# A transformer megakernel on one Trainium2 core: the two local-attention layers as one pipeline over tiles, with the inverse norm taken by a power on GpSimd

## The reference

```python
def _layer(x, wqkv, qs, ksc, wo, lg, lb, w1, b1, w2, b2):
    h = shift_token(x)
    q, k, v = jnp.split(h @ wqkv, 3, axis=-1)       # then to 8 heads
    q = l2norm(q) * qs
    k = l2norm(k) * ksc
    q, k = rotary_xpos(q, k)
    o = local_attention(q, k, v)                    # windows of 64, each sees itself and the one before, softmax
    x = x + o @ wo
    h = shift_token(x)
    ...                                             # layer norm, gated MLP
```

## Time and profile before

| | |
|---|---|
| median of 3 runs | 3057.51 us (3056.97 to 3065.76) |
| the profiled execution, its own time | 3055.92 us |
| its span, first to last instruction | 3054.1 us |
| instructions | 46022 |
| mean granted TensorE clock | 0.847 of 2.4 GHz |

### The profile page before, as it was taken

One profiled execution on the slowest core, in us unless ns is written; L12 is line 12 of the kernel. 1 busy time (PEld: TensorE's weight loads), 2 busy tenths in 40 slices (PEclk: granted clock), 3 DMA queues, 4 the chain that ended last, 5 costly groups with the idle time before them and its releaser, 6 DMA issues.

```text
span 3054.1 us, 46022 instructions
## 1 busy us (share of the span) xinstructions
PE 2275.5 (75%) x17392; PEld 1277.1 (42%) x17392; DVE 1975.2 (65%) x4104; ACT 1416.0 (46%) x2537; POOL 560.6 (18%) x336
## 2 busy tenths in 40 slices
PE   4798588577779668767759948867767985885766
PEld 4576122254547412245546712225353751222545
DVE  5855696655674489565656568946566556966565
ACT  1333277264533347554623416746263332782544
POOL 0242000213043200041205300012212420003130
PEclk9999599778879879978779968978777985997878
DMA  3000200101000100010000020010100002001010
GB/s 132 1 1 1 74 16 9 28 6 26 11 9 1 53 22 19 8 27 11 21 17 1 1 69 19 7 22 16 22 17 8 1 1 74 16 9 30 5 26 18
DMA packets 52016, 65.13 MB, mean 21 GB/s; under 512 B 17696, under 2 KB 29216, under 8 KB 51264
## 3 DMA queue, kind: packets, MB, share of 16 engines
q1 hardware_dynamic: 48584, 56.18, 7.3%
q10 hardware_dynamic: 3192, 5.80, 0.6%
HBM read 25.19 MB, written 15.01 MB: 13 GB/s over the span
## 4 chain that ended last, share of the span: by engine, by line
PE 49%; DVE 23%; ACT 12%; DMA 6%; issue 5%; SPq 3%; POOL 2%; ACTq 0%; DVEq 0%; POOLq 0%
PE PS L1136 44%; DVE arena L971 9%; ACT arena L616 5%; DMA tmp<-xf 3%; ACT arena L571 2%; PE PS L1415 2%; PE PS L1154 1%; DVE s_at L1027 1%; DMA scr_k<-arena 1%; DVE tmp L996 1%; POOL arena L437 1%; DMA arena<-scr_k 1%; PE PS L1480 1%; SPq L344 1%; DVE arena L1044 1%
## 5 line engine op out<-in xcount | busy, mean ns | idle before, releaser
L1136 PE MATMUL PS<-arena 128*32 128x256 f32 (+4 forms) x10240 | 825.3, 356 | 204.4 <-DMA arena<-scr_k 75.3
L971 DVE TENSOR_REDUCE arena<-PS 128x1 f32<-128x512 f32 x1024 | 642.0, 684 | 101.7 <-PE PS L1136 101.7
L571 ACT ACTIVATE arena<-PS 128x1024 f32<-128x1024 f32 x512 | 515.6, 1033 | 306.7 <-PE PS L1136 306.7
L1136 PEld LDWEIGHTS PS<-arena 128*32 128x32 f32 (+4 forms) x10240 | 313.0, 124 | 714.9 <-DVE arena L971 282.9
L1136 PE MATMUL PS<-wqkv,arena 128*128 128x512 f32 x384 | 221.1, 730 | 65.4 <-ACT arena L602 56.2
L1136 PEld LDWEIGHTS PS<-w2e,arena 128*128 128x128 f32 x2048 | 246.0, 192 | 52.0 <-issue 51.7
L527 ACT ACTIVATE arena<-PS 128x512 f32<-128x512 f32 x256 | 150.7, 597 | 245.1 <-PE PS L1136 245.0
L1136 PE MATMUL PS<-w2e,arena 128*128 128x128 f32 x2048 | 246.8, 275 | 0.1
L616 ACT ACTIVATE arena<-PS,arena 128x128 f32<-128x128 f32 x512 | 230.0, 527 | 16.0 <-DVE arena L1079 16.0
L917 DVE TENSOR_TENSOR arena<-PS,arena 128x512 f32<-128x512 f32 x128 | 86.1, 689 | 213.2 <-PE PS L1136 212.8
L601 ACT ACTIVATE arena<-PS 128x1024 f32<-128x1024 f32 x64 | 65.5, 1023 | 325.1 <-DVE s_at L1027 248.5
(11 more groups left out here) (274 smaller groups left out, 3463.7 us busy)
## 6 DMA issues: line engine op xcount, KB each, us to landing
arena<-arena SPq DMA_DIRECT2D x120, 128.0 KB, 2.3
arena<-scr_k SPq DMA_DIRECT2D x28, 200.0 KB
arena<-scr_q SPq DMA_DIRECT2D x28, 192.0 KB
scr_q<-arena SPq DMA_DIRECT2D x16, 256.0 KB, 3.0
scr_k<-arena SPq DMA_DIRECT2D x16, 256.0 KB, 5.2
x_in<-in_x SPq DMA_DIRECT2D x5, 512.0 KB, 4.0
scr_q<-arena ACTq DMA_DIRECT2D x8, 256.0 KB, 4.9
scr_k<-arena ACTq DMA_DIRECT2D x8, 256.0 KB, 5.8
```

Source lines behind the costliest of these rows:

```text
L571: act.activation(pb[:, n % 8], pair(2 * (n % 2)), ACT.Exp).then_inc(S["p"], 1)
L971: dve.tensor_reduce(mxp[:, h % 2, j, t, hf:hf + 1], PS[:, ring_bank("mx", h, n), :], AX, ALU.max)\
L1136: return pe.matmul(o, w, v, start=start, stop=stop, **kw)
```

## The change

The two phases become one loop of steps j. In step j the engines work on the projections of tile j+3, the norms and transposes of tile j+2, the scores of tile j+1, the exponentials of tile j, the division and transposition of j-1, and the output of j-3; j runs from -3. The PSUM banks are shared otherwise: scores have the one pair 0, 1, q and k the one pair 2, 3, v bank 4, the transposes of q, k and of the probabilities banks 5 and 6 in turn, output and projection bank 7. `qT` is held for two tiles, `pl` for two, `qk_a` for two and `qk_sq` for one. ACT copies both halves of the transposed probabilities. SP's two loops become one; `vz` has a semaphore for each tile, and `qk_ps` is new, so SP clears eight more semaphores at the end of an item.

The inverse norm of one tile is taken by one POOL instruction (sum to the power -0.5, 16 values per partition; the exponent comes from `sc[:, 11:12]`, set once), and DVE refines it with one Newton step. ACT's square root and DVE's reciprocal go, so do ACT's table loads for the square root (one per layer) and, in layer 0, the one for the exponential (the stage before ends in exponentials).

The diff, cut to its core:

```diff
-        qT = take([4, N])
-        after = used[0]
-        pl = take([3, 2, 4, KEYS])
+        pl = take([2, 2, 4, KEYS])
         pt = take([2, 2, 4, P])
+        hT = take([N])
+        qk_a = [take([2 * INNER]) for _ in range(2)]
+        qk_sq = take([2 * INNER])
         olT = x_in[:].rearrange("p (q c) n -> p q c n", c=4)
-        part = [take([2 * INNER], F32, after + i * 2 * INNER) for i in range(4)]
-        hT = take([N], F32, after + 4 * 2 * INNER)
-        flat = [v[:].rearrange("p t w -> p (t w)") for v in (tmp, x_in, s_at, tmp2)]
-        qk_a = part[0:2] + flat[0:2]
-        qk_b = flat[2:4]
-        qk_sq = part[2:4]
...
+                    for j in range(-3, T):
+                        t, u = j + 2, l * T + j + 2
+                        if 0 <= t < T:
+                            pool.wait_ge(S["ssq_ok"], u + 1)
+                            pool.tensor_tensor(rq[:, t], ssq[:, t], sc[:, 11:12].broadcast_to([P, 2 * HL]), ALU.pow).then_inc(S["rq0"], 1)
+                            pool.wait_ge(S["rot"], u + 1)
+                            pool.wait_ge(S["rqe"], u + 1)
+                            v = qk_a[u % 2][:, INNER:].rearrange("p (h c) -> p h c", c=DL)
+                            pool.tensor_tensor(v, v, bc(rq[:, t, HL:], [P, HL, DL], 2), ALU.mult).then_inc(S["qkr"], 1)
+                        t, u = j + 3, l * T + j + 3
+                        if 0 <= t < T:
+                            v = qk_a[u % 2]
                             pool.wait_ge(S["rotb"], u + 1)
                             pool.tensor_tensor(v, v, qk_b[u % 2], ALU.add).then_inc(S["rot"], 1)
-                        if t >= 2:
-                            k = u - 2
-                            pool.wait_ge(S["rot"], k + 1)
...
+                    def exps(t):
+
+                        n = l * T + t
+                        act.wait_ge(S["ml"], n + 1)
+                        if n >= 2:
+                            act.wait_ge(S["pt_ps"], 2 * (n - 1))
+                        for r in range(2):
+                            for c in range(4):
+                                h = 2 * c + r
+                                act.activation(pl[:, n % 2, r, c], PS[:, r, KEYS * c:KEYS * c + KEYS],
+                                               ACT.Exp, bias=ml[:, n % 2, r, c:c + 1], scale=rq[:, t, h:h + 1],
+                                               accum_out=sl[:, n % 3, r, c:c + 1]).then_inc(S["p_exp"], 1)
+
+                    for j in range(-3, T + 3):
+                        if 0 <= j < T:
+                            exps(j)
+                        t, u = j - 3, l * T + j - 3
+                        if 0 <= t < T:
+                            act.wait_ge(S["o_lps"], u + 1)
+                            if u >= 2:
+                                act.wait_ge(S["ol_ps"], u - 1)
+                            act.copy(olT[:, u % 2], PS[:, 7, :].rearrange("p (c n) -> p c n", c=4)).then_inc(S["olT"], 1)
+                        t, u = j - 2, l * T + j - 2
+                        if 0 <= t < T:
+                            if u >= 2:
+                                act.wait_ge(S["o_lps"], u - 1)
+                            for r in range(2):
+                                act.wait_ge(S["pt_ps"], 2 * u + r + 1)
...
+                        if 0 <= t < T:
+                            act.wait_ge(S["qkv_ps"], u + 1)
+                            act.copy(vl[:, t], PS[:, 4, :]).then_inc(S["vl"], 1)
+                        t, u = j + 2, l * T + j + 2
+                        if 0 <= t < T:
+                            act.wait_ge(S["kq_ps"], 2 * u + 1)
+                            if t >= 2:
+                                act.wait_ge(S["s_lps"], u - 1)
+                            act.copy(qT[:, t % 2], PS[:, 5, :].rearrange("p (c n) -> p c n", c=4)).then_inc(S["kq"], 1)
+                            act.wait_ge(S["kq_ps"], 2 * u + 2)
+                            act.copy(kT[:, :, WIN + P * t:WIN + P * t + P],
+                                     PS[:, 6, :].rearrange("p (c n) -> p c n", c=4)).then_inc(S["kq"], 1)
+                        t, u = j + 3, l * T + j + 3
+                        if 0 <= t < T:
                             act.wait_ge(S["rotb"], u + 1)
-                            if u >= 2:
-                                act.wait_ge(S["ssq"], u - 1)
-                            act.activation(qk_sq[u % 2], pair(2 * (t % 2)), ACT.Square).then_inc(S["sq"], 1)
-                            act.copy(vl[:, t], PS[:, 4 + t % 2, :]).then_inc(S["vl"], 1)
-                        if 2 <= t <= T and t % 2 == 0:
-                            k = t - 2
-                            act.wait_ge(S["ssq_ok"], u // 2)
-                            act.activation(rqt[:, k:k + 2], ssq[:, k:k + 2], ACT.Sqrt).then_inc(S["rq0"], 1)
...
+                    def norms(t):
+
                         u = l * T + t
-                        if t < T:
-                            rotate(t)
-                        if t >= 1:
-                            k = t - 1
-                            dve.wait_ge(S["sq"], u)
-                            dve.tensor_reduce(ssq[:, k], qk_sq[(u - 1) % 2].rearrange("p (h c) -> p h c", c=DL),
-                                              AX, ALU.add).then_inc(S["ssq"], 1)
-                        if 2 <= t and t % 2 == 0:
-
-                            k = t - 2
-                            y, v, w = rq[:, k:k + 2], ssq[:, k:k + 2], rqt[:, k:k + 2]
-                            dve.wait_ge(S["ssq"], u)
-                            dve.tensor_scalar(v, v, 1e-24, None, ALU.max).then_inc(S["ssq_ok"], 1)
-                            dve.wait_ge(S["rq0"], u // 2)
-                            link(dve.reciprocal(y, w))
-                            link(dve.scalar_tensor_tensor(w, y, -0.5, y, ALU.mult, ALU.mult))
-                            link(dve.tensor_tensor(w, w, v, ALU.mult))
-                            dve.scalar_tensor_tensor(y, w, 1.5, y, ALU.add, ALU.mult).then_inc(S["rqe"], 2)
+                        y, v, w = rq[:, t], ssq[:, t], rqt[:, t]
+                        dve.wait_ge(S["sq"], u + 1)
+                        dve.tensor_reduce(v, qk_sq.rearrange("p (h c) -> p h c", c=DL), AX, ALU.add).then_inc(S["ssq"], 1)
+                        dve.wait_ge(S["ssq"], u + 1)
+                        dve.tensor_scalar(v, v, 1e-24, None, ALU.max).then_inc(S["ssq_ok"], 1)
+                        dve.wait_ge(S["rq0"], u + 1)
+                        link(dve.scalar_tensor_tensor(w, y, -0.5, y, ALU.mult, ALU.mult))
+                        link(dve.tensor_tensor(w, w, v, ALU.mult))
+                        dve.scalar_tensor_tensor(y, w, 1.5, y, ALU.add, ALU.mult).then_inc(S["rqe"], 1)
+
+                    def divide(t):
+
+                        m = l * T + t
+                        dve.wait_ge(S["p_exp"], 8 * (m + 1))
+                        link(dve.reciprocal(rl[:, m % 3], sl[:, m % 3]))
+                        v = pl[:, m % 2]
+                        dve.tensor_tensor(v, v, bc(rl[:, m % 3], [P, 2, 4, KEYS], 3), ALU.mult).then_inc(S["pn"], 1)
+
+                    def maximum(t):
+
+                        n = l * T + t
+                        sv = PS[:, 0:2, :].rearrange("p r (c k) -> p r c k", k=KEYS)
+                        dve.wait_ge(S["s_lps"], n + 1)
+                        if n >= 2:
+                            dve.wait_ge(S["p_exp"], 8 * (n - 1))
+                        dve.wait_ge(S["rqe"], n + 1)
+                        link(dve.tensor_reduce(ml[:, n % 2], sv, AX, ALU.max))
+                        dve.scalar_tensor_tensor(ml[:, n % 2], ml[:, n % 2], -1.0,
+                                                 rq[:, t, 0:HL].rearrange("p (c r) -> p r c", r=2),
+                                                 ALU.mult, ALU.mult).then_inc(S["ml"], 1)
 
...
+                    for j in range(-3, T + 4):
+                        t = j - 4
+                        if 0 <= t < T:
                             dve.wait_ge(S["ol_ps"], l * T + t + 1)
                             dve.tensor_tensor(xf[:, t], xs[:, t], PS[:, 7, 0:W], ALU.add).then_inc(S["xf"], 1)
                             if t:
                                 own_half(t - 1)
                             if t >= 2:
                                 late_stats(t - 2)
-                        if 3 <= u <= T + 2:
-                            m = n - 3
-                            if m >= 2:
-                                dve.wait_ge(S["o_lps"], m - 1)
-                            dve.wait_ge(S["pt_ps"], 2 * m + 2)
-                            dve.tensor_copy(pt[:, m % 2, 1], PS[:, 5, :].rearrange("p (c n) -> p c n", c=4))\
-                                .then_inc(S["ptd"], 1)
+                        if 0 <= j + 2 < T:
+                            norms(j + 2)
+                        if 0 <= j - 1 < T:
+                            divide(j - 1)
+                        if 0 <= j + 3 < T:
+                            rotate(j + 3)
```

(64 more changed lines are left out.)

186 lines of the change are left out of this document (51 added, 135 removed).

## The result

The changed kernel takes 3133.51 us in the median (4 runs, 3124.72 to 3134.09), the kernel before 3057.24 beside it: ratio 1.0239, 95% interval 1.0211 to 1.0267. The forecast was 3044 with a range up to 3118; the time lies above it. It is slower, as in rival 1, "the power is slow".

What follows compares the result with a forecast made beforehand. No engine was full: a dependent chain bound phase one, ACT phase two. DVE's operations, stands and the power's wait made 10.6 us a full step, 101.5 a layer; saving 13.6 us gave 3044, range 2976 to 3118.

Steps and rivals of the forecast that it cites:

- rival 1: POOL's power is slow and DVE stands in its queue for it: 3104 at 2 us, 3164 at 3; chance 0.22.
- the term P: DVE's wait for POOL's power in a full step: 1.0 us for the instruction, 0.17 for two hand-overs, 1.17 us.
- The law around it: About 7.5 steps of a layer carry the power, so each us of it costs 60 us in all.
- The maximum is held: The maximum's last DVE operation stands for POOL's addition, ending 2.5 us after the rotation where 1.42 would do.
- The division is not held: The forecast had DVE's division held by POOL's scaling, ending 2.35 us behind the norms instead of 1.45.
- Rival 4: PE runs at half the clock in full steps, its share 15.6 us against 10.6: 3140 us; chance 0.10.
- the 1.1 for `zz`: Layer 0: POOL's two big `zz` operations fall between scaling 7 and maximum 6, which stands for one: 1.1 us lost.
- the start: First steps of a layer, from POOL's first addition: tile 1's maximum was to end at 26.8 us.
- Rival 2: POOL's power is quick: at 0.5 us the kernel takes 3014 us; chance 0.17.
- Rival 3: DVE and POOL don't collide in division and maximum: steps of 8.6 us, 2976 us in all; chance 0.12.
- Rival 5: The hand-made schedule misses a wait; no price given; chance 0.04.

Runs made afterwards that it cites:

- the product: The changed kernel with POOL's power replaced by a product of the same 16 values with a constant: 2986.49 us, ratio 0.9776.
- half the power: The changed kernel with the power on only 8 of 16 values per partition, a product on the other 8: 3060.46 us.

## Why the prediction was wrong

**The step that failed is the term P.** The estimate for the power was 1.0 us; it takes 2.905. The nearest row below was ACT's root of 32 values, 0.24 us, and the forecast took a value close to the low end, though its own higher case, "a hundred times" an addition's price per value, gave 3.7 us. Measured it is 0.158 us a value against 0.0023 for the addition: 69 times. With nothing in the trace between the ends, nothing spoke for 1.0; the middle of the ends would have been about 2. And the price of the other way stood in the trace: the kernel before takes the inverse roots of its layer norms on DVE, from the same seed with three Newton steps, in operations of 0.17 us each:

```profile
L733 DVE TENSOR_TENSOR nr_t<-nr_t,var 128x8 f32<-128x8 f32 (+1 forms) x111 | 18.3, 165 | 3.8
```

**The law around it held.** "Each us of it costs 60 us": 54.7 by the product, and 53 by half the power in the steps of its profiled execution (69 by the medians, for the reasons above). It is under 60 because the first steps of a layer don't pay in full: in layer 0 of item 4 the product makes the first and third 1.1 and 1.9 us shorter for 2.69 us less of POOL. Put into the forecast, 3044 + 60 x 1.905 = 3158; measured 3133.5. And with 0.215 us it gives 3044 - 47 = 2997; measured 2986.5. So the base of 3044 was sound to about 10 us at that end, and 25 too high at the other. That it was sound is in part luck, as shown below. The range to 3118 cut off a power above 2.2 us, and that was the case.

**The maximum is held**: forecast 2.5 us from the rotation's end to the maximum's, measured 2.46 (2888.03 to 2890.49), L1064 taking 1.29 where it takes 0.16 with the addition done. Shown by the version that puts the sum there.

**The division is not held.** Forecast 2.35 us from Newton's end to where the rotation follows; it took 1.29 (2884.33 to 2885.62), and POOL's scaling was the one to give way:

```profile
2884.48 1.23 DVE L1053 TENSOR_TENSOR arena<-arena 128x1024 f32<-128x1024 f32 x1
```

```profile
2884.47 2.13 POOL L432 TENSOR_TENSOR arena<-arena 128x512 f32<-128x512 f32 x1 [0.77 <-DVE arena L1045]
```

The collision is real, 2.13 for 1.04, but it fell on the engine that had time. That makes a full step 1.1 us shorter than forecast: 10.6 + 1.905 - 1.1 = 11.4, measured 11.1; the other 0.3 is spread over Newton (0.60 for 0.72), the sum and the hand-overs. The version with the division beside the power has POOL's scaling at 1.04 again. The Trainium skill (page "SBUF — State Buffer", section "Who interferes with whom") has the pair of SBUF ports that VectorE and GpSimd share as an exclusive lock: for the addition and the scaling the traces agree, one of the two stretches by about the other's time; beside the power the division ran its 1.24 us at once, so there the measurement decides against a lock for the whole instruction.

**Rival 4, PE cold**, was placed in the full steps, and there it did not occur: from the fourth step on the granted clock was 0.82 to 1.00 in all eight layers, and the step was 11.1, 11.1, 11.3 and 11.4 us at each of them. It came in the tail, from the last power of a layer to the last statistics. Steps repeat to 0.02 us between items, but the tail of layer 0 was 35.1 us in item 1, 40.8 in item 2, 40.7 in item 3 and 36.6 in item 4. The whole tails of items 1 and 2:

```profile
640.82:675.91 35.09, 23.05 (x324) 20.06 (x324) 16.87 (x37) 18.43 (x60) 9.70 (x4) 0.90 0.03 7
1394.49:1435.27 40.78, 28.03 (x324) 24.59 (x324) 16.29 (x37) 18.43 (x60) 9.69 (x4) 0.75 0.03 6
```

The chain of work settles what the difference is. In both tails it has 8.29 us of ACT, 5.06 of POOL, 1.7 of DVE and 2.2 of issue, but 17.76 us of PE in item 1 and 23.46 in item 2, the same instructions at a granted clock of 0.90 and 0.75. The difference of 5.7 us is PE's alone. Why the clock was lower in one item than in another stays open. In layer 1 the tails are 35.3 to 38.2 us.

The forecast had 31.2 us for this tail with the 1.1 for `zz`, 33.1 with the dear power: 2 to 8 us too little a layer. The part ahead of it was forecast too long: 75.4 us from the first addition to the last power, where the forecast's working gives 71.4, or 84.7 with the dear power. Of these 9.3 us, 4.2 are the division that was not held, in four steps, 3.4 the start (tile 1's maximum ends at 29.1 us, where the working with the dear power gives 32.5), and the rest 0.3 to 0.4 a step. Two errors of opposite sign stood behind a sum for layer 0 that came out 5 us too high (102.6 with the `zz`, 116.9 with 7.5 powers at 1.905 us more, 112.05 measured). That they nearly cancel is luck.

**Rival 2** fell with the power; the product's run shows what it would have paid, 68 us under the kernel before. **Rival 3** was half right: the division isn't held, the maximum is, and with the sum put into that stand the changed kernel wins 52 us. Rival 5: no wait was missing.

## What to carry to other kernels

Before an operation is given to another engine, ask what one value costs there and who waits while it runs. A function that looks like one instruction may cost 70 times an addition per value, and on an in-order queue its latency is paid in every turn of the loop; splitting or batching doesn't help when the price goes by the value, while nine small operations on the engine itself, 0.21 us each, were cheaper. Look first whether the kernel already does the same elsewhere: here its own layer norms had the cheaper way.

Where a price has no row, the range must reach its upper bound if the time hangs on it at 60 to 1, and the value to take is between the ends, not the one next to a familiar operation.

A wait can be filled with other work of the same queue, but look at each moved instruction from both sides: is its input ready that early (the rotation's wasn't), and who now stands behind it (the exponentials behind the sum)? A new order can also tie a step to an engine that had slack before, and then to that engine's clock.

## What the runs showed of the hardware

POOL's power takes 1.65, 2.91 and 5.43 us for 8, 16 and 32 values a partition, 0.38 + 0.158 for each, where a product of 16 takes 0.22 and one of 8 takes 0.20. A DVE division of 1024 columns beside the power is undisturbed. When POOL's scaling and DVE's division start within 0.01 us, DVE's ran at its normal 1.23 us and POOL's took 2.13 instead of 1.04; when POOL's addition is under way first, DVE's operation stands for it. So POOL won where its addition was under way first, and DVE at the tie; other orders are not shown here. Two SBUF inputs are not needed for such a stand: the clamp of the earlier trace rows has one, and in the changed kernel a DVE copy of 128x64 from SBUF to SBUF (L1071, at 2922.90) takes 2.33 us beside POOL's 2.34 us on `zz`, where it takes 0.18 alone. DVE's sum of 1024 columns, also with one, is not held.
